# Redrawn issue orders on all five engines of a windowed-attention, depthwise-convolution and MLP block

## The chip, the cores and the metric

The kernel runs on one core of a Trainium2 chip. The metric is the device time of one execution in microseconds (us), as the median of several; less is better. TensorE (PE) does the matmuls, VectorE (DVE), ScalarE (ACT) and GpSimd (POOL) the elementwise work, SyncE (SP) issues most of the DMA transfers. PEld is TensorE's loading of weights, which runs beside its matmuls.

## The reference

The input is 32 images of 96 channels and 56 x 56 pixels. The block is attention in windows of 7 x 7 tokens with 12 heads of 8 channels, a residual sum, a depthwise 3 x 3 convolution with batch norm, and an MLP with 384 hidden channels and a second residual sum.

```python
xw = x.reshape(B, C, 8, 7, 8, 7) ...        # windows of 49 tokens
xn = layernorm(xw) * g + b
q, k, v = xn @ qkv_w.T + qkv_b
attn = softmax(q * SCALE @ k.T + bias)      # 12 heads, 49 x 49 each
seq = x + (attn @ v) @ proj_w.T + proj_b
seq2 = batchnorm(depthwise_conv3x3(seq))
out = seq2 + gelu(seq2 @ w1.T + b1) @ w2.T + b2
```

## The kernel before

The work is cut into 256 chunks. A chunk is one band of seven image rows: 8 windows, 392 tokens (`CT`). Windows are taken in four pairs, so scores, exponentials and values come in four groups, `p` = 0 to 3. There is no scheduler: each engine has a loop over `STEPS` steps whose body is a list of calls written out by hand, such as `exp_scores(s - 4, 2)`, which in step `s` issues the group for chunk `s - 4`. A chunk that doesn't exist (`real(c)` false) issues nothing. An engine runs its list strictly in that order, and engines wait for each other on semaphores: `wait(eng, s, c)` waits until the event `s` of chunk `c` has come, and `free(eng, ...)` until the last reader of a buffer has finished. The step number of one engine has no fixed relation to that of another; only the waits tie them.

What one chunk issues on TensorE, with the line that records it:

- `centred` (L255, writes `d_ps`) and `variance` (L363, `b_ps`): the LayerNorm as two fp32 matmul groups; ScalarE squares (L533) between them, and takes logarithm and root behind them (L540, L547). VectorE multiplies (`input_normal`, L810), ScalarE and GpSimd split the result into two fp16 parts (`input_high` L555, `input_low` L599).
- `queries` (L255, `a_ps`), `keys` (L255, `b_ps`), `values` (L266 to L268, `a_ps`): three fp16 products each. ScalarE and VectorE evict queries and keys as high and low parts (`query_high`, `key_high`, `query_low`, `key_low`), and SP lays them out by six transfers a chunk (`term`, L213).
- `max_scores` (L320, `sm_ps`, four groups): scores whose row maxima VectorE takes (`maxima`, L738). `maxima_rows` (L329) transposes the maxima, VectorE copies them out (`maxima_out`, L748) and SP places them (`maximum_row`, L225).
- `exp_scores` (L299, `st_ps`, four groups): the scores again, transposed, with the maximum subtracted; ScalarE takes the exponential (`exp`, L474).
- `values_times_p` (L345, `o_ps`, four groups): values times exponentials. ScalarE evicts two groups at a time (`outputs`, L499), GpSimd issues four transfers (`to_channels`, L637), ScalarE inverts the sums and VectorE multiplies (`normalise`, L755).
- `projection` (L399, `b_ps`); VectorE adds the residual (`image_sum`, L820). The convolution's nine taps follow, two on GpSimd and seven on VectorE (`tap`, L764).
- `hidden` k = 0, 1, 2 (L266 to L268 into `d_ps`, `a_ps`, `b_ps`), `gelu` on ScalarE (L525), and `second` k = 0, 1, 2 (L255), which accumulates in `d_ps`; VectorE adds up the output (`block_out`, L801) and SP stores it (`store`).

Each of the score and value groups is 24 matmul records with 24 weight loads, 49 columns wide each: 48 instructions. The long groups have few: `centred` 8, `variance` 4, `projection` 8, `keys` and `queries` 12 each, one `hidden` 6, one `second` 8, `values` 24, `maxima_rows` 2. The three scalar calls of a step that need the exponential's table and the three that need the GELU's are separated by two table loads (L560, L574).

`st_ps` and `sm_ps` (two banks each) have one home, so a group of scores can be issued only when the one before it has been read. `a_ps`, `b_ps`, `d_ps` (one bank each) go round between the long groups.

Of the kernel before, what the change touches and what calls it, by code (L numbers as in the profile page):

```python
# [33 lines left out]
STEPS = CHUNKS + 11  # L34
# [4 lines left out]
def block_program(nc, x, w_qkv, b_qkv_row, b_v, w_proj, w_proj_rows, b_proj, ln_g, ln_b, bias_q,  # L39
                  conv_w, bn_g, bn_b, bn_mean, bn_var, w1, b1, w2, b2, eye, low, half, out):  # L40
    ctx = ExitStack()
    with ctx:
# [138 lines left out]
        def _(sp):  # L181
# [51 lines left out]

            for s in range(STEPS):
                load(s)
                first_term(k_all, 0, kh, kh_done, s - 3)
                term(k_all, 2, kh, kh_done, s - 3)
                term(q_all, 0, qh, qh_done, s - 3)
                term(q_all, 2, ql, ql_done, s - 3)
                term(k_all, 1, kl, kl_done, s - 3)  # L240
                term(q_all, 1, qh, qh_done, s - 3)
                store(s - 11)
                maximum_row(s - 4)
# [5 lines left out]
        def _(pe):  # L249
# [82 lines left out]
            def values_times_p(c, p):  # L332
                if not real(c):
                    return
                if p == 0:
                    wait(pe, v32_done, c)
                wait(pe, p_done[p], c)
                if p == 0:
                    free(pe, (o_done[1], c-1), (o_done[0], c-1))
                elif p == 2:  # L340
                    free(pe, (o_done[0], c), (o_done[1], c-1))
# [62 lines left out]
            def hidden(c, k):  # L404
# [3 lines left out]
                if k == 0:  # L408
# [9 lines left out]
            def second(c, k):  # L418
# [6 lines left out]
                halves(d_ps[0:128, 0:CT], w2_s[:, k, :], g[:, k, :], start=k == 0, stop=k == 2).then_inc(s_done[k], 1)  # L425

            for s in range(STEPS):
                exp_scores(s - 4, 2)
                max_scores(s - 3, 3)
                projection(s - 6)  # L430
                hidden(s - 8, 0)
                maxima_rows(s - 3)
                hidden(s - 8, 1)
                hidden(s - 8, 2)
                exp_scores(s - 4, 3)
                max_scores(s - 2, 0)
                second(s - 8, 0)
                second(s - 8, 1)
                second(s - 8, 2)
                keys(s - 1)  # L440
                max_scores(s - 2, 1)
                queries(s - 1)
                exp_scores(s - 3, 0)
                centred(s)
                max_scores(s - 2, 2)
                exp_scores(s - 3, 1)
                values_times_p(s - 4, 2)
                values_times_p(s - 4, 3)
                variance(s)
                values(s - 2)  # L450
                values_times_p(s - 3, 0)
                values_times_p(s - 3, 1)
# [4 lines left out]
        def _(act):  # L457
# [34 lines left out]
            def outputs(c, half):  # L492
# [3 lines left out]
                wait(act, pv_done[1 if half == 0 else 3], c)  # L496
# [5 lines left out]
            def key_high(c):  # L502
# [3 lines left out]
                wait_ring(act, exp_in, c - 2, 6 * 16)  # L506
# [4 lines left out]
            def query_high(c):  # L511

                if not real(c):
                    return
                wait(act, q_done, c)
# [381 lines left out]
```

## Time and profile before

| | |
|---|---|
| median of 3 runs | 3189.77 us (3189.08 to 3205.73) |
| the profiled execution | 3164.1 us |
| its span, first to last instruction | 3162.3 us |
| busy: PE, DVE, ACT, POOL | 96%, 91%, 88%, 62% |
| first and last transpose of maxima (L329), one a chunk | 66.1 and 3104.1 us |

The busy share says how much of the span an engine had an instruction in flight; instructions overlap on an engine, so the sum of the durations of its instructions is above its busy time. "issue" as a reason for idleness means that the engine waited for nothing that the profile shows: no semaphore and no transfer of the program.

### The profile page before, as it was taken

How to read it: one execution, taken by the hardware profiler on the slowest of the kernel's cores; microseconds unless marked ns; L12 is line 12 of the kernel's file. 1: busy time of each engine (PE TensorE's matmuls, PEld its weight loads, DVE VectorE, ACT ScalarE, POOL GpSimd, SP SyncE). 2: the span in 40 equal slices, each digit the busy share in tenths (PEclk: the TensorE clock that was granted, in tenths of full speed). 3: DMA queues.
4: the chain of work that ended last, by engine and by line, in shares of the span. 5: the costliest groups of instructions: out<-in, count | busy, mean ns of one | idle time of the engine just before them, and what ended most of it. 6: DMA issues, size and time to landing. Idle time of an engine off the chain costs nothing.

```text
span 3162.3 us, 199772 instructions
## 1 busy us (share of the span) xinstructions
PE 3029.4 (96%) x88076; PEld 2105.9 (67%) x88076; DVE 2888.8 (91%) x4908; ACT 2768.5 (88%) x4867; POOL 1956.6 (62%) x2574
## 2 busy tenths in 40 slices
PE   3899999999999999999999999999999999999997
PEld 2666666666766666666666666666666676666663
DVE  4799999999999999999999999999999999999996
ACT  2799999989989999998989999988989999998986
POOL 2566666666666666666666666666666666666664
PEclk9999999999999999999999999999999999999998
DMA  1233333333333333333333333333333333333331
GB/s 40 86 91 96 91 96 94 92 95 91 97 91 94 95 94 95 96 91 95 91 96 94 94 96 94 92 96 91 95 95 93 96 97 93 95 98 91 95 92 41
DMA packets 269922, 288.31 MB, mean 91 GB/s; under 512 B 55651, under 2 KB 252580, under 8 KB 269062
## 3 DMA queue, kind: packets, MB, share of 16 engines
q1 hardware_dynamic: 236294, 198.40, 22.6%
q0 software_dynamic: 32768, 77.14, 7.0%
q8 instruction: 700, 11.47, 1.5%
q14 instruction: 160, 1.31, 0.1%
HBM read 39.34 MB, written 38.54 MB: 25 GB/s over the span
## 4 chain that ended last, share of the span: by engine, by line
PE 91%; issue 3%; ACT 2%; SPq 1%; DMA 1%; DVE 1%; POOL 0%; POOLq 0%; ACTq 0%; DVEq 0%
PE d_ps L255 21%; PE st_ps L299 12%; PE o_ps L345 11%; PE sm_ps L320 10%; PE b_ps L363 7%; PE b_ps L399 6%; PE a_ps L255 4%; PE b_ps L255 4%; PE a_ps L266 3%; PE a_ps L268 3%; PE a_ps L267 3%; PE d_ps L266 1%; PE d_ps L268 1%; PE b_ps L267 1%; PE d_ps L267 1%
## 5 line engine op out<-in xcount | busy, mean ns | idle before, releaser
L764 DVE SCALAR_TENSOR_TENSOR s<-ximg,cols,s 96x392 f32<-96x392 f32 x1792 | 1137.0, 635 | 30.7 <-POOL s L627 3.2
L738 DVE TENSOR_REDUCE mx<-sm_ps 128x12 f16<-128x588 f32 x1024 | 785.0, 767 | 127.7 <-PE sm_ps L320 125.1
L474 ACT ACTIVATE p<-st_ps 128x588 f32<-128x588 f32 x1024 | 672.4, 657 | 179.2 <-PE st_ps L299 176.1
L637 POOL DMA_DIRECT2D ox<-o_sb x1024 | 582.7, 572 | 30.8 <-ACT o_sb L499 17.2
L320 PEld LDWEIGHTS sm_ps<-k_all,q_all 127*49 127x49 f16 x24576 | 460.6, 104 | 171.5 <-issue 76.0
L255 PE MATMUL d_ps<-g,w_s 128*64 128x392 f32 x3072 | 560.2, 500 | 0.0
L299 PEld LDWEIGHTS st_ps<-q_all,k_all 128*49 128x49 f16 x24576 | 435.5, 103 | 157.2 <-issue 107.8
L610 POOL TENSOR_TENSOR s<-ximg,cols 96x392 f32<-96x392 f32 x256 | 216.0, 844 | 520.5 <-DVE y L801 519.9
L299 PE MATMUL st_ps<-q_all,k_all 128*49 128x49 f16 x24576 | 516.1, 186 | 21.4 <-issue 19.3
L320 PE MATMUL sm_ps<-k_all,q_all 127*49 127x49 f16 x24576 | 508.6, 186 | 25.9 <-issue 15.6
L599 POOL TENSOR_TENSOR xl<-xn,xh 96x392 f16<-96x392 f32 x256 | 258.8, 1011 | 273.6 <-ACT xh L555 256.5
L645 POOL CAST sh<-s 96x392 f16<-96x392 f32 x256 | 199.5, 779 | 350.0 <-DVE s L764 350.0
L345 PE MATMUL o_ps<-p,v 128*32 128x49 f32 x24576 | 384.9, 209 | 15.2 <-issue 13.1
L345 PEld LDWEIGHTS o_ps<-p,v 128*32 128x32 f32 x24576 | 308.9, 110 | 48.8 <-issue 18.8
L560 ACT ACT_TABLE_LOAD x256 | 328.4, 1283 | 4.5
L574 ACT ACT_TABLE_LOAD x256 | 328.4, 1283 | 4.4
L255 PEld LDWEIGHTS d_ps<-g,w_s 128*64 128x64 f32 x3072 | 197.2, 137 | 197.0 <-ACT g L525 116.0
L791 DVE TENSOR_TENSOR v<-a_ps,half_c 128x768 f32<-128x768 f32 x256 | 245.1, 958 | 36.1 <-PE a_ps L268 16.2
L627 POOL TENSOR_TENSOR s<-s,part 96x392 f32<-96x392 f32 x256 | 261.2, 1020 | 0.1
L652 POOL TENSOR_TENSOR sl<-s,sh 96x392 f16<-96x392 f32 x256 | 239.8, 937 | 20.5
L255 PE MATMUL d_ps<-x_sb,center 96*64 96x392 f32 x1024 | 224.1, 516 | 20.9 <-DMA x_sb<-in_x 20.9
L399 PE MATMUL b_ps<-ox,wp 96*96 96x196 f32 x1024 | 233.3, 350 | 6.3 <-DVE ox L755 5.6
(122 smaller groups left out, 5959.7 us busy)
## 6 DMA issues: line engine op xcount, KB each, us to landing
ox<-o_sb POOLq DMA_DIRECT2D x1024, 73.5 KB
k_all<-kh SPq DMA_DIRECT2D x512, 75.0 KB
q_all<-qh SPq DMA_DIRECT2D x512, 75.0 KB
x_sb<-in_x SPq DMA_DIRECT2D x256, 147.0 KB, 2.4
out<-y SPq DMA_DIRECT2D x256, 147.0 KB, 2.7
q_all<-ql SPq DMA_DIRECT2D x256, 75.0 KB
k_all<-kl SPq DMA_DIRECT2D x256, 75.0 KB
q_all<-mxt SPq DMA_DIRECT2D x256, 9.4 KB, 2.1
```

What stands on the lines that cost most here:

```text
L255: last = mm(o[64 * h:64 * h + 64], w[:, 64 * h:64 * h + 64], m, start=start, stop=stop)
L299: last = mm(st_ps[64 * w:64 * w + TOK, h // HH, c0:c0 + TOK], k_all[:, r, h, n:n + TOK], q_all[:, r, h, n:n + TOK], start=True, stop=True)
L320: last = mm(sm_ps[64 * w:64 * w + TOK, h // HH, c0:c0 + TOK], q_all[0:MAXROW, r, h, n:n + TOK], k_all[0:MAXROW, r, h, n:n + TOK], start=Tr ...
L345: last = mm(o_ps[32 * c4:32 * c4 + 32, at:at + TOK], v32[:, c % 2, h, p, :], p32[:, p, h, :], start=True, stop=True)
L399: last = mm(o, wp[:, 0:C], ox[:, c % 2, w, :].rearrange("c (n r k) -> c n r k", n=NP, k=WS), start=True, stop=True)
L474: af(p32[:, p, :, :].rearrange("p (b h) n -> p b h n", b=2), st_ps[:, :, 0:HALF].rearrange("p b (h n) -> p b h n", n=TOK), ACT.Exp).then_i ...
L560: act.preload_act_table_set("natural_log_exp_and_others")
L574: act.preload_act_table_set("gelu_and_others")
L627: tt(acc, acc, image(part[:, :]), ALU.add).then_inc(tap_done[1], 1)
L637: nc.gpsimd.dma_start(ox[:, c % 2, x4, :], o_sb[x4::4, c % 2, :, :]).then_inc(o_in[c % 2], 16)
L738: v.tensor_reduce(mx[:, c % 2, 0:HEADS, p].rearrange("p (b h) -> p b h", b=2), sm_ps[:, :, 0:HALF].rearrange("p b (h n) -> p b h n", n=TOK ...
L764: v.scalar_tensor_tensor(acc, image_rows(c, k // 3, k % 3), cw_c[:, k:k + 1], acc, ALU.mult, ALU.add)\
```

## The change

The five lists are drawn up anew. On TensorE the eight score groups and the four value groups are spread between the long groups in another order; `values_times_p` takes its pairs in the order 3, 2 and 1, 0; the accumulation in `d_ps` takes `second` in the order 0, 2, 1, with the last of them in the step after; `values` comes before `variance`. The waits move with them (`v32_done` and `o_done` at p = 1 and 3, `pv_done[0]` and `[2]`, `sl_done` at k = 1, `s_done[1]`, the wait for `exp_in` from `key_high` to `query_high`). ScalarE, GpSimd, VectorE and SP get orders and step offsets that go with it. No operation is added or removed, and no shape or buffer changes; `hidden` keeps its PSUM homes.

```diff
...
 CROW = WS * PAD
-STEPS = CHUNKS + 11
+STEPS = CHUNKS + 9
 UP = 256.0
...
             for s in range(STEPS):
+                first_term(q_all, 0, qh, qh_done, s - 2)
+                store(s - 9)
+                term(q_all, 1, qh, qh_done, s - 2)
+                term(k_all, 2, kh, kh_done, s - 2)
+                term(q_all, 2, ql, ql_done, s - 2)
+                term(k_all, 1, kl, kl_done, s - 2)
+                term(k_all, 0, kh, kh_done, s - 2)
                 load(s)
-                first_term(k_all, 0, kh, kh_done, s - 3)
-                term(k_all, 2, kh, kh_done, s - 3)
-                term(q_all, 0, qh, qh_done, s - 3)
-                term(q_all, 2, ql, ql_done, s - 3)
-                term(k_all, 1, kl, kl_done, s - 3)
-                term(q_all, 1, qh, qh_done, s - 3)
-                store(s - 11)
-                maximum_row(s - 4)
+                maximum_row(s - 3)
             for r in stored:
...
                     return
-                if p == 0:
+                if p == 1:
                     wait(pe, v32_done, c)
                 wait(pe, p_done[p], c)
-                if p == 0:
+                if p == 1:
                     free(pe, (o_done[1], c-1), (o_done[0], c-1))
-                elif p == 2:
+                elif p == 3:
                     free(pe, (o_done[0], c), (o_done[1], c-1))
...
                     return
-                if k == 0:
+                if k == 1:
                     wait(pe, sl_done, c)
...
                     free(pe, (g_done[0], c), (xn_done, c+7), (y_done, c-1))
-                halves(d_ps[0:128, 0:CT], w2_s[:, k, :], g[:, k, :], start=k == 0, stop=k == 2).then_inc(s_done[k], 1)
+                halves(d_ps[0:128, 0:CT], w2_s[:, k, :], g[:, k, :], start=k == 0, stop=k == 1).then_inc(s_done[k], 1)
...
             for s in range(STEPS):
-                exp_scores(s - 4, 2)
-                max_scores(s - 3, 3)
-                projection(s - 6)
-                hidden(s - 8, 0)
-                maxima_rows(s - 3)
-                hidden(s - 8, 1)
-                hidden(s - 8, 2)
-                exp_scores(s - 4, 3)
-                max_scores(s - 2, 0)
-                second(s - 8, 0)
-                second(s - 8, 1)
-                second(s - 8, 2)
-                keys(s - 1)
                 max_scores(s - 2, 1)
                 queries(s - 1)
+                second(s - 8, 1)
                 exp_scores(s - 3, 0)
+                keys(s - 1)
+                max_scores(s - 2, 2)
+                values_times_p(s - 4, 3)
+                values_times_p(s - 4, 2)
                 centred(s)
-                max_scores(s - 2, 2)
                 exp_scores(s - 3, 1)
-                values_times_p(s - 4, 2)
-                values_times_p(s - 4, 3)
+                values(s - 2)
                 variance(s)
-                values(s - 2)
+                exp_scores(s - 3, 2)
+                max_scores(s - 2, 3)
+                values_times_p(s - 3, 1)
                 values_times_p(s - 3, 0)
-                values_times_p(s - 3, 1)
+                projection(s - 5)
+                hidden(s - 7, 1)
+                maxima_rows(s - 2)
+                hidden(s - 7, 0)
+                hidden(s - 7, 2)
+                exp_scores(s - 3, 3)
+                max_scores(s - 1, 0)
+                second(s - 7, 0)
+                second(s - 7, 2)
...
                     return
-                wait(act, pv_done[1 if half == 0 else 3], c)
+                wait(act, pv_done[0 if half == 0 else 2], c)
                 if half == 0:
...
                     return
-                wait_ring(act, exp_in, c - 2, 6 * 16)
                 wait(act, k_done, c)
...
                     return
+                wait_ring(act, exp_in, c - 2, 6 * 16)
                 wait(act, q_done, c)
...
             for s in range(STEPS):
-                gelu(s - 8, 2)
                 if real(s - 8):
...
                 exp(s - 4, 3)
-                key_high(s - 1)
                 query_high(s - 1)
...
                 log_sums(s - 5)
+                key_high(s - 1)
+                inverses(s - 5)
                 square(s)
-                inverses(s - 5)
                 exp(s - 3, 1)
...
                 log_variance(s)
+                exp(s - 3, 2)
                 root(s)
-                exp(s - 3, 2)
                 if real(s - 7):
                     act.preload_act_table_set("gelu_and_others")
+                gelu(s - 7, 1)
                 gelu(s - 7, 0)
+                input_high(s)
+                gelu(s - 7, 2)
                 outputs(s - 3, 0)
-                input_high(s)
-                gelu(s - 7, 1)
...
             for s in range(STEPS):
+                second_product(s - 6)
                 first_product(s - 6)
-                second_product(s - 6)
                 image_high(s - 7)
...
                 wait(dve, v_done, c)
-                wait(dve, pv_done[3], c - 2)
+                wait(dve, pv_done[2], c - 2)
                 v.tensor_tensor(v32[:, c % 2, :, :, :].rearrange("p h n (d x) -> p (h n d) x", x=4)[:, :, 0:2],
...
                     return
-                wait(dve, s_done[2], c)
+                wait(dve, s_done[1], c)
                 dve.wait_ge(stored[c % 2], (c // 2 + 1) * 16)
...
             for s in range(STEPS):
-                maxima(s - 2, 2)
+                key_low(s - 1)
+                tap(s - 7, 7)
+                tap(s - 7, 8)
+                normalise(s - 5)
                 values_out(s - 2)
+                maxima(s - 2, 3)
                 input_normal(s)
-                maxima(s - 2, 3)
                 image_sum(s - 5)
...
                 tap(s - 6, 5)
+                maxima(s - 1, 1)
                 tap(s - 6, 6)
                 block_out(s - 7)
-                maxima(s - 1, 1)
-                key_low(s)
                 query_low(s)
-                tap(s - 6, 7)
-                tap(s - 6, 8)
-                normalise(s - 4)
+                maxima(s - 1, 2)
...
```

## Rows read from the trace of the kernel before

**Rows 1.** The page: busy time and share of each engine; the queue of instruction packets.

```profile
PE 3029.4 (96%) x88076; PEld 2105.9 (67%) x88076; DVE 2888.8 (91%) x4908; ACT 2768.5 (88%) x4867; POOL 1956.6 (62%) x2574
...
q8 instruction: 700, 11.47, 1.5%
```

**Rows 2.** Line L329, one matmul a chunk: duration min/median/max, first and last start.

```profile
L329 PE MATMUL sm_ps<-eye_h,mx x256: 219/221/343, 66.1 to 3104.1; 128*96 128x128 f16 x128
```

**Rows 3.** The page, groups: busy, mean ns | idle before, releaser.

```profile
L299 PE MATMUL st_ps<-q_all,k_all 128*49 128x49 f16 x24576 | 516.1, 186 | 21.4 <-issue 19.3
L320 PE MATMUL sm_ps<-k_all,q_all 127*49 127x49 f16 x24576 | 508.6, 186 | 25.9 <-issue 15.6
...
L345 PE MATMUL o_ps<-p,v 128*32 128x49 f32 x24576 | 384.9, 209 | 15.2 <-issue 13.1
```

**Rows 4.** Timeline of PE over one chunk: start, duration, engine, line, operation.

```profile
1512.70 0.33 PE L268 MATMUL b_ps<-sh,w_l 96*128 96x392 f16 x1
1512.96 0.50 PE L299 MATMUL st_ps<-q_all,k_all 128*49 128x49 f16 x24
...
1513.63 2.17 PE L255 MATMUL d_ps<-g,w_s 128*64 128x392 f32 x12
...
1517.31 0.86 PE L255 MATMUL d_ps<-x_sb,center 96*64 96x392 f32 x4
1518.00 0.49 PE L320 MATMUL sm_ps<-k_all,q_all 127*49 127x49 f16 x24
1518.32 0.48 PE L299 MATMUL st_ps<-q_all,k_all 128*49 128x49 f16 x24
1518.73 0.73 PE L345 MATMUL o_ps<-p,v 128*32 128x49 f32 x48
1519.39 0.90 PE L363 MATMUL b_ps<-sq,avg 96*96 96x392 f32 x2
1520.13 0.21 PE L266 MATMUL a_ps<-wq_h,xh 96*128 96x96 f16 x1
...
1520.59 0.21 PE L268 MATMUL a_ps<-wq_h,xl 96*128 96x96 f16 x1
1520.73 0.73 PE L345 MATMUL o_ps<-p,v 128*32 128x49 f32 x48
1521.39 0.50 PE L299 MATMUL st_ps<-q_all,k_all 128*49 128x49 f16 x24
...
1522.14 0.90 PE L399 MATMUL b_ps<-ox,wp 96*96 96x196 f32 x4
1522.88 0.33 PE L266 MATMUL d_ps<-sh,w_h 96*128 96x392 f16 x1
...
1524.53 0.24 PE L299 MATMUL st_ps<-q_all,k_all 128*49 128x49 f16 x4
```

**Rows 5.** Timeline of PE at a pause in a score group, 1545 to 1547 us.

```profile
1545.35 0.34 PE L320 MATMUL sm_ps<-k_all,q_all 127*49 127x49 f16 x13
1546.49 0.29 PE L320 MATMUL sm_ps<-k_all,q_all 127*49 127x49 f16 x9 [0.79 <-issue]
```

**Rows 6.** DMA queues from 1543.5 to 1543.7 us: packets, MB, share of 16 engines.

```profile
q8 instruction: 1, 0.02, 44.8%
```

**Rows 7.** Timeline of ACT over the same chunk.

```profile
1511.05 1.28 ACT L574 ACT_TABLE_LOAD   x1
...
1515.91 0.66 ACT L474 ACTIVATE p<-st_ps 128x588 f32<-128x588 f32 x1
...
1520.33 0.58 ACT L540 ACTIVATE sq<-b_ps,cols 96x392 f32<-96x392 f32 x1
1520.94 0.53 ACT L547 ACTIVATE sq<-sq 96x392 f32<-96x392 f32 x1
```

**Rows 8.** Timeline of DVE: residual sum, and the maxima that end the stretch.

```profile
1511.52 0.62 DVE L820 SCALAR_TENSOR_TENSOR ximg<-b_ps,cols,x_sb 96x392 f32<-96x392 f32 x1
...
1513.91 0.76 DVE L738 TENSOR_REDUCE mx<-sm_ps 128x12 f16<-128x588 f32 x1
```

## The prediction

> **What bounds the kernel now.** I read the page first. TensorE is busy for 96% of the span, the others for less [rows 1]; busy is not the same as running at its best, so I went on to the spacing of the groups. The transposes of the maxima come once a chunk: (3104.1 - 66.1) / 255 = 11.91 us for a chunk [rows 2]. Then the timeline of TensorE over one chunk in which nothing is late: from one fourth exponential group to the next, 1512.96 to 1524.53, are 11.57 us, and every group starts as soon as the one before it lets it [rows 4]. So 0.34 us of a chunk, 88 us of the run, are pauses, and the rest is the list itself. The groups of the page say what the pauses are: of 21.4, 25.9 and 15.2 us of idle time before score and value matmuls, 19.3, 15.6 and 13.1 are "issue", no semaphore and no transfer of the program [rows 3]. (The modelled ends hide about 0.2 us of each pause, so these 48 us stand for most of the 88.)
>
> One pause shows the cause. A group of maximum scores stops after 13 of its 24 matmuls and goes on 0.79 us later, at 1546.49 [rows 5]; a matmul in the middle of a group has nothing of the program to wait for. Between 1543.5 and 1543.7 an instruction packet starts; its 44.8% of 16 engines over 0.2 us are 1.4 us of transfer [rows 6]. The queue carries 700 packets and 11.47 MB, 16 KB each [rows 1]. TensorE's 176,152 matmuls and weight loads and some 3,000 semaphore instructions make 700 times 256. So a packet is a block of 256 instructions. I count 256 back from the restart: 26 of this group, 48, 96, 24, 4, and 58 of the 96 of `values_times_p`. By the pitches of [rows 4] that stretch would take 0.18 + 0.34 + 0.66 + 0.60 + 0.74 + 0.40 = 2.9 us; it took 3.9. I read it so: a new block is asked for when the block before is entered, and is ready some 3.1 to 3.9 us later. A stretch of 256 instructions that the array could do faster than that ends in a pause. The mean block has 11.91 / 2.73 = 4.4 us; the dense ones don't.
>
> The Trainium skill ("Runtime: NRT & Kernel Launch", Instruction fetch mechanics) says that instructions are refilled in 16 KiB blocks of 256, which the queue's packets agree with, and that crossing a block's edge is mostly hidden, which the 0.79 us above speaks against. It is a rival below.
>
> **The change, part by part.** Nothing is added or removed, so only order counts.
>
> *Dense stretches.* Before, `max_scores` 2, `exp_scores` 1, `values_times_p` 2 and 3, `variance`, `values`, `values_times_p` 0 and 1, `exp_scores` 2 and `max_scores` 3 follow each other: 412 instructions from 1518.00 to 1522.14, 4.14 us [rows 4], which is 2.6 to 2.9 us for any 256 of them. Now `centred`, `exp_scores` 1, `values`, `variance`, `exp_scores` 2, `max_scores` 3, `values_times_p` 1 and 0 make the densest stretch. From `exp_scores` 1 on, 256 instructions (48, 24, 4, 48, 48, 84 of 96) take 0.41 + 0.54 + 0.81 + 0.34 + 0.41 + 0.57 = 3.1 us; those from `max_scores` 2 on take 3.7, all others more. I slide a window of 256 instructions over the 700 starts of a chunk's list, each group's time spread evenly over its instructions. Before, 36% of the starts lie below 3.3 us, and 700 blocks lose 95 us at a refill of 3.3 us (46 at 3.1, 176 at 3.6). The 88 us measured fit 3.27. The same sliding over the new list gives 11% of the starts and 12 us at 3.3 (3 at 3.1, 40 at 3.6). As refills scatter, I take 17 us, with 5 and 40 as ends. Gain 71 us (48 to 83).
>
> *Edges between groups.* TensorE pays when it goes from one width of output to another. I call A the groups on 64 columns (scores, `centred`, `queries`, `keys`, `second`), B those on 32 (`values_times_p`), C those on 96 or 128. From [rows 4]: C to A costs 0.26 - 0.17 = 0.09 and 0.02 in the group behind; A to B 0.41 - 0.32 = 0.09; B to C 0.74 - 0.66 = 0.08; C to B 0.60 for twelve matmuls that start (1520.59 - 1520.13) / 11 = 0.042 apart, 0.10; B to A 0.02; A to C 0.75 + 0.74 against 0.66 + 0.66, 0.17. Each stands once in the old list: 0.57. The new list has A-B (`max_scores` 2), B-A (`centred`), A-C (`exp_scores` 1 to `values`), C-A (`variance` to `exp_scores` 2), A-B (`max_scores` 3), B-C (`projection`) and C-A (`hidden` 2): seven edges. A-C into fp16 is not in the trace: 0.09 to 0.17, between which I take 0.13. `variance` behind `values` isn't either: its fp32 weights load behind matmuls of 0.04 us, 0 to 0.08, I take 0.04. Sum 0.09 + 0.02 + 0.13 + 0.04 + 0.11 + 0.09 + 0.08 + 0.11 = 0.67. `second` in two pieces pays its start twice: one pair of halves like `centred` takes 0.69 to the next group, each further pair (2.17 - 0.86) / 2 = 0.655, so 0.03. The list without pauses is 11.57 + 0.67 - 0.57 + 0.03 = 11.70 us (11.62 to 11.78): 256 x 0.13 = 33 us lost (12 to 54).
>
> *Waits that could reach TensorE.* I laid the new lists beside each other at 11.70 us with `max_scores` 1 at 0. Three places have little room.
> ScalarE: from `variance` (5.07) the way goes back to `exp_scores` 0 of the next step. Start of `variance` to the logarithm 0.94 [rows 4, 7]; logarithm to the exponential group behind it 0.47 to 0.61; this group and the root 0.55 each; from the first table load to the exponentials behind the second 4.86, as the same three GELUs, one output eviction and `input_high` stand between them in both lists [rows 7]; the exponential group 0.66 and a semaphore 0.05. That is 8.08 to 8.22, and 8.35 if the group behind the logarithm takes its full 0.66 and more. TensorE's own list from `exp_scores` 0 to `variance` is 3.56. The loop is 11.64 to 11.78, at worst 11.91, beside TensorE's 11.70.
> VectorE: `projection` starts at 7.27; its result is there 0.95 later; `image_sum`, `tap` 2, `maxima_out`, `tap` 3 and 4 take 2.39, `maxima` 0 another 0.76, and 0.05 [rows 8]: 4.15 us, and `max_scores` 1, which needs it, comes 4.42 us after `projection`. Spare 0.27. VectorE is busy 2888.8 / 256 = 11.3 us of a chunk [rows 1], so it stays under 11.70 but has nothing to give.
> GpSimd and SP: `input_low` ends some 0.5 us before `queries`. SP blocks in order: behind `maximum_row`'s wait stand the next chunk's six transfers, but their data comes 4 us later, so nothing is held up; with some 0.7 us an issue, and the store now ahead of five of them, the last of the six still goes out about 4 us before `max_scores` 0 needs it. The load of x goes out 5 us earlier relative to its use.
> For all of these I add 5 us (0 to 30, the end where the loop is 11.80).
>
> *Pipeline depth.* `STEPS` falls by two, but this renumbers more than it shortens. From `centred` to the transpose were 3 steps less 5.4 us, now 2 steps and 5.1; from there to the last `second` 5 steps and 3.8, now 5 and 4.7. Both within 1 us: 0, with 8 either way.
>
> *Sum.* -71 + 33 + 5 + 0 = -33 us. The profiled execution took 3164.1 us (a span of 3162.3 and 1.8 around it), so 3131 by its own time. The median of the runs is 3189.8, 0.8% above; taking the difference over as it is, I predict 3157 us.
>
> **The rivals.**
> *1. The ScalarE loop sets the pace, slower.* It would replace the pauses by a wait of `exp_scores` 0 for `exp` 3. For it: the loop is within 0.1 us of TensorE's list at the lower rows, 11.91 at the highest. Against: ACT has idle time before a chunk's `exp` groups now, and is busy 2768.5 / 256 = 10.8 us [rows 1]. At 11.91 with 0.07 of pauses it is 11.98, and 256 x 0.07 = +18 us, 3208. From a loop of 11.91 on it ends as slower than 3206.
> *2. The pauses stay.* The Trainium skill's rule on block edges stands beside this one: if an edge of a block were hidden, the issue time would have another cause, which the order would not touch. As a mechanism of this kernel: the pauses come at the same rate, 88 us, and the edges add 33: 3223. Against: the pause in the middle of a group and the count of 256.
> *3. Everything is used up.* The high ends of both: refills so slow that the pauses fall by only 48, edges that take 54, waits 5: 3201, no change to speak of.
> *4. More than I say.* The low ends of both, the edges and the refill: -83 + 12: 3119.
>
> **How the numbers follow.** Less than 0.5% (16 us) is about what a measurement of this kernel can't tell from no change. The forecast with rival 4, below 3174, 0.65; rival 3 and mixtures that end between 3174 and 3206, 0.18; rival 1 0.09; rival 2 0.08. The forecast's own range is 3127 to 3180, from the ends of its terms short of all falling together. For 8 in 10 the range goes down to rival 4 and up past rival 1: 3115 to 3210.
>
> **What would show it.** Right: transposes 11.75 to 11.80 us apart; undisturbed chunks at 11.62 to 11.78; "issue" before L299, L320 and L345 well under half of 48 us; `values` to `variance` and `exp_scores` 2 as costed. Wrong: `exp_scores` 0 waiting for `exp` (L474), `max_scores` 1 for `maxima` (L738), `queries` for `input_low` (L599), or issue time as before.

## The result: 1.3% slower, and the profile after

The changed kernel takes 3234.9 us (median of 4 runs, 3229.1 to 3241.6) where the kernel before takes 3191.9 on the same chip: 1.0127, 95% interval [1.009, 1.0163]. The profiled execution took 3229.1 us, 65.0 more than the one of before. The forecast was 3157 us and faster. A second measure of the same kernel on another occasion (a_again below) gave 1.014. The page of the changed kernel:

```profile
PE 3065.0 (95%) x88076; PEld 2093.7 (65%) x88076; DVE 2871.7 (89%) x4908; ACT 2745.1 (85%) x4867; POOL 2039.4 (63%) x2574
...
q8 instruction: 700, 11.47, 1.6%
...
L299 PE MATMUL st_ps<-q_all,k_all 128*49 128x49 f16 x24576 | 522.9, 186 | 31.3 <-issue 27.2
L320 PE MATMUL sm_ps<-k_all,q_all 127*49 127x49 f16 x24576 | 510.3, 185 | 30.0 <-DMA k_all<-kh 12.2
...
L345 PE MATMUL o_ps<-p,v 128*32 128x49 f32 x24576 | 382.3, 209 | 22.6 <-issue 21.5
```

Beside [rows 1, 3]: the same 700 instruction packets. TensorE and GpSimd are busy for longer (3065.0 us beside 3029.4, 2039.4 beside 1956.6), VectorE and ScalarE for less, and as a share of the span none moved by more than three points. The issue time before exponential scores rose from 19.3 to 27.2 us and before values from 13.1 to 21.5. The prediction wanted well under half of 48. The transposes, from the query on L329:

```profile
L329 PE MATMUL sm_ps<-eye_h,mx x256: 219/221/257, 65.7 to 3169.2; 128*96 128x128 f16 x128
```

(3169.2 - 65.7) / 255 = 12.17 us a chunk, against 11.91 [rows 2]. Head and tail of the run are as before (65.7 and 58.1 us beside 66.1 and 58.2), so the whole loss lies between them. First, a chunk in which nothing is late (timeline of TensorE):

```profile
660.09 0.22 PE L329 MATMUL sm_ps<-eye_h,mx 128*96 128x128 f16 x1
...
665.58 0.50 PE L320 MATMUL sm_ps<-k_all,q_all 127*49 127x49 f16 x24
666.01 0.73 PE L345 MATMUL o_ps<-p,v 128*32 128x49 f32 x48
666.67 0.88 PE L255 MATMUL d_ps<-x_sb,center 96*64 96x392 f32 x4
667.38 0.49 PE L299 MATMUL st_ps<-q_all,k_all 128*49 128x49 f16 x24
667.80 0.22 PE L266 MATMUL a_ps<-wq_h,xh 96*128 96x96 f16 x1
...
668.32 0.86 PE L363 MATMUL b_ps<-sq,avg 96*96 96x392 f32 x2
669.11 0.50 PE L299 MATMUL st_ps<-q_all,k_all 128*49 128x49 f16 x24
669.45 0.48 PE L320 MATMUL sm_ps<-k_all,q_all 127*49 127x49 f16 x24
669.86 0.73 PE L345 MATMUL o_ps<-p,v 128*32 128x49 f32 x48
670.52 0.90 PE L399 MATMUL b_ps<-ox,wp 96*96 96x196 f32 x4
...
671.76 0.22 PE L329 MATMUL sm_ps<-eye_h,mx 128*96 128x128 f16 x1
```

671.76 - 660.09 = 11.67 us; the kernel before has 11.56 at its best. So the edges between groups cost 0.11 x 256 = 29 us, where 33 were forecast for them and the two pieces of `second`: `values` to `variance` 0.52, `variance` to `exp_scores` 2 0.79, the whole list within 0.03 of the 11.70 on record. That part was right.

The rest is 12.17 - 11.67 = 0.50 us a chunk that is not in the list, where before it was 0.36. To split it I went through TensorE's records in order (matmuls, weight loads, semaphore instructions) and cut them into blocks of 256. In both traces the unexplained gaps in the middle of groups fall on one fixed remainder, the first instruction of a block. A "pause" below is what the spacing at such an edge of a block has over the same place in undisturbed chunks, and a block is "entered" when the array starts its first instruction. Summed over all edges the pauses are **86 us before (189 of them) and 103 us after (188)**; 94 in the second execution of the changed kernel. The forecast was 17. Besides, waits for transfers of k_all and q_all, for `input_low` and for `maxima` rose: in TensorE's waits those for `k_all` (12.2), `q_all` (0.9), `xl` (10.1) and `mx` (6.7 and 1.1) make 31 us, and before 16. List 29, pauses 17 and these 15 make 61 of the 65 us.

What the new pauses look like. This is TensorE's timeline around the worst kind, then the one row of ScalarE there, then the queues from 1750.4 to 1750.6 us:

```profile
1747.94 0.48 PE L320 MATMUL sm_ps<-k_all,q_all 127*49 127x49 f16 x24
...
1748.78 0.83 PE L255 MATMUL d_ps<-g,w_s 128*64 128x392 f32 x4
1749.47 0.50 PE L299 MATMUL st_ps<-q_all,k_all 128*49 128x49 f16 x24
...
1750.31 0.50 PE L320 MATMUL sm_ps<-k_all,q_all 127*49 127x49 f16 x24
1750.74 0.72 PE L345 MATMUL o_ps<-p,v 128*32 128x49 f32 x47
1753.17 0.20 PE L345 MATMUL o_ps<-p,v 128*32 128x49 f32 x1 [1.70 <-issue]
```

```profile
1748.67 0.66 ACT L474 ACTIVATE p<-st_ps 128x588 f32<-128x588 f32 x1
```

```profile
q8 instruction: 1, 0.02, 40.8%
```

The block that ends in this pause began in `max_scores` 1, at about 1748.05 (counted back from the pause: 94 instructions of `values_times_p`, 48 of `max_scores` 2, 12 of `keys`, 48 of `exp_scores` 0, 8 of `second`, 12 of `queries`, some six semaphore instructions, and the last 28 of `max_scores` 1). The next packet starts in 1750.4 to 1750.6: some 2.4 us after the block was entered, where in [rows 5, 6] it was about 1. It takes 0.408 x 16 x 0.2 = 1.3 us, and work goes on 1.4 us after it has landed, as elsewhere. Late is only its start. And that start lies 1.1 us behind the end of the exponential of group 3 (1748.67 + 0.66 = 1749.33), for which `exp_scores` 0 waits, some 50 instructions behind the first of the block. That exponential is rival 1's. It costs the array nothing here: `exp_scores` 0 starts at 1749.47, on the heels of `second`.

### The profile page after: what moved, and what is told of

The parts are those of the page before. It is cut to its first block, busy times and chain, and to the rows that moved or that the text cites. A ratio compares the mean times of both kernels' runs of the same rounds, so it can differ in the third digit from the quotient of the medians.

```text
span 3227.3 us, 199772 instructions
## 1 busy us (share of the span) xinstructions
PE 3065.0 (95%) x88076; PEld 2093.7 (65%) x88076; DVE 2871.7 (89%) x4908; ACT 2745.1 (85%) x4867; POOL 2039.4 (63%) x2574
## 4 chain that ended last, share of the span: by engine, by line
PE 86%; issue 4%; DMA 3%; SPq 3%; ACT 2%; DVE 2%; POOL 1%; POOLq 0%; ACTq 0%; DVEq 0%
PE d_ps L255 21%; PE st_ps L299 11%; PE o_ps L345 10%; PE sm_ps L320 10%; PE b_ps L399 6%; PE b_ps L363 5%; PE a_ps L255 4%; PE b_ps L255 4%; PE a_ps L266 3%; PE a_ps L268 2%; PE a_ps L267 2%; DMA k_all<-kh 2%; SPq L213 2%; PE d_ps L266 1%; PE d_ps L267 1%
## 5 line engine op out<-in xcount | busy, mean ns | idle before, releaser
L299 PEld LDWEIGHTS st_ps<-q_all,k_all 128*49 128x49 f16 x24576 | 447.4, 103 | 495.1 <-issue 330.0
L255 PE MATMUL d_ps<-g,w_s 128*64 128x392 f32 x3072 | 603.7, 500 | 0.1
L299 PE MATMUL st_ps<-q_all,k_all 128*49 128x49 f16 x24576 | 522.9, 186 | 31.3 <-issue 27.2
L320 PE MATMUL sm_ps<-k_all,q_all 127*49 127x49 f16 x24576 | 510.3, 185 | 30.0 <-DMA k_all<-kh 12.2
L345 PE MATMUL o_ps<-p,v 128*32 128x49 f32 x24576 | 382.3, 209 | 22.6 <-issue 21.5
L599 POOL TENSOR_TENSOR xl<-xn,xh 96x392 f16<-96x392 f32 x256 | 270.7, 1058 | 159.1 <-ACT xh L555 150.8
L345 PEld LDWEIGHTS o_ps<-p,v 128*32 128x32 f32 x24576 | 307.4, 110 | 37.9 <-issue 18.0
L618 POOL TENSOR_TENSOR part<-ximg,cols 96x392 f32<-96x392 f32 x256 | 289.0, 1129 | 0.2
L533 ACT ACTIVATE sq<-d_ps 96x392 f32<-96x392 f32 x256 | 126.0, 492 | 148.8 <-PE d_ps L255 148.8
```

What stands on the lines that cost most here:

```text
L255: last = mm(o[64 * h:64 * h + 64], w[:, 64 * h:64 * h + 64], m, start=start, stop=stop)
L299: last = mm(st_ps[64 * w:64 * w + TOK, h // HH, c0:c0 + TOK], k_all[:, r, h, n:n + TOK], q_all[:, r, h, n:n + TOK], start=True, stop=True)
L320: last = mm(sm_ps[64 * w:64 * w + TOK, h // HH, c0:c0 + TOK], q_all[0:MAXROW, r, h, n:n + TOK], k_all[0:MAXROW, r, h, n:n + TOK], start=Tr ...
L345: last = mm(o_ps[32 * c4:32 * c4 + 32, at:at + TOK], v32[:, c % 2, h, p, :], p32[:, p, h, :], start=True, stop=True)
L599: tt(xl[0:C, c % 2, :, 0:TOK], xn[:, :, :], xh[0:C, c % 2, :, 0:TOK], ALU.subtract).then_inc(xl_done, 1)
L618: tt(image(part[:, :]), image_rows(c, 0, 1), weight(1), ALU.mult).then_inc(part_done, 1)
```

## The experiments

Pauses in the table are counted as above, from one trace a kernel; two traces of the same kernel gave 103 and 94 us, so a difference of some 10 us is not one. "List" is the undisturbed chunk. Each ratio is to the kernel before on the same chip; names with b_ are edits of the kernel before, with a_ of the changed one.

| kernel | ratio, 95% interval | list, us | pauses at edges of blocks, us (number) |
|---|---|---|---|
| before | 1 | 11.56 | 86 (189) |
| changed | 1.0127 [1.009, 1.0163] | 11.67 | 103 (188) |
| a_again | 1.014 [1.0114, 1.0165] | 11.67 | 94 (184) |
| b_thin | 0.9808 [0.9787, 0.9829] | 11.55 | 32 (68) |
| a_thin | 0.9914 [0.989, 0.9937] | 11.72 | 9 (20) |
| b_lite | 0.9959 [0.9942, 0.9976] | 11.56 | 86 (193) |
| a_lite | 1.0107 [1.0081, 1.0133] | 11.67 | 92 (168) |
| a_thin1 | 1.0449 [1.0421, 1.0478] | 11.68 | 187 (270) |
| a_thin2 | 0.9934 [0.9908, 0.9959] | 11.69 | 19 (48) |
| b_thin2 | 0.9856 [0.9826, 0.9886] | 11.56 | 56 (122) |
| a_thin1_notab | 0.9938 [0.9914, 0.9962] | 11.65 | 39 (77) |
| a_notab | 0.9934 [0.9916, 0.9952] | 11.65 | 40 (76) |
| b_notab | 1.0137 [1.0116, 1.0158] | 11.56 | 130 (233) |
| a_swap | 1.0064 [1.0041, 1.0086] | 11.65 | 77 (131) |
| b_low | 0.999 [0.9975, 1.0006] | 11.56 | 94 (207) |
| b_notab_low | 0.9932 [0.991, 0.9953] | 11.56 | 92 (200) |
| a_swap2 | 0.9951 [0.9935, 0.9967] | 11.65 | 47 (111) |
| a_swap2_again | 0.9988 [0.9974, 1.0002] | 11.65 | 49 (104) |
| b_later | 1.0645 [1.0621, 1.067] | 12.50 | 53 (119) |

**Is it the number of instructions? b_thin and a_thin.** In every `max_scores` group four matmuls of 384 columns stand for 24 of 49, so 8 instructions for 48 in the same time; the maxima are of other products then, and the exponential's scale is 0.01. In both kernels:

```
-                for h in range(HEADS):
+                for b in range(2):
                     for w in range(2):
...
+                        last = mm(sm_ps[64 * w:64 * w + TOK, b, 0:384], q_all[0:MAXROW, r, b, n:n + TOK],
+                                  k_all[0:MAXROW, r, b, 0:384], start=True, stop=True)
```

> The kernel before, but each max_scores group is 4 matmuls of 384 columns (8 instructions) in the place of 24 of 49 (48 instructions), about the same 0.32 us of the array; the maxima are of other scores, and the exponential is taken of a hundredth of its argument. A chunk has 540 instructions, not 700. Refill theory (pauses come when TensorE runs through a block of 256 instructions faster than the next arrives): a block lasts 5.6 us on the mean, nearly all pauses go, 11.6 us a chunk, 3060 to 3100 us by the profiled time. Rival, the pauses have another cause (waits, edges of groups): 3140 to 3165 as before.

> The changed kernel with the same thinning of max_scores. Refill theory: pauses nearly gone here too, what is left is the undisturbed list, 11.67 us a chunk in its own trace against 11.56: 3085 to 3125 us by the profiled time, 25 to 40 us above the thinned kernel before, so about 80 of the change's 110 us of pauses and list are pauses. Rival, the new lists wait on ScalarE or VectorE: it stays above 3180.

Pauses fell from 86 to 32 and from 103 to 9 us with a list unchanged in one and 0.05 longer in the other. TensorE's waits of a_thin show hardly any issue time left:

```profile
PE st_ps L299 <- issue: 3.5, 10, 0.6
```

The profiled execution of b_thin took 3104.7 us, 5 above its expectation, that of a_thin 3144.9, 20 above: TensorE's waits for k_all (12.5 us) and for `input_low` (13.7 us) stay in a_thin. The pauses are refills in both kernels, against rival 2; what is wrong is the size they were given.

**Is it the traffic that slows a packet? b_lite and a_lite.** The transfers of the terms move one of eight windows; the rest of the scores' operands stays as it was set at the start.

```
-                sp.dma_start(t[n:TERMS:4, c % 4, :, :], part[:, c % 2, :]).then_inc(exp_in[c % 4], 16)
+                sp.dma_start(t[n:TERMS:4, c % 4, :, 0:KP], part[:, c % 2, 0:KP]).then_inc(exp_in[c % 4], 16)
```

> The kernel before with the six transfers of queries and keys a chunk moving one of eight windows (9 KB each in the place of 75); the other windows' scores are those of the initial tables. Traffic theory (the instruction packet waits behind and beside the program's own transfers): refills shorten by 0.3 us or more and most of the 88 us of pauses go: 3090 to 3110. Density theory (the packet needs its time whatever else moves): at most 20 us less, 3140 to 3160.

> The changed kernel with the same small transfers. Traffic theory, by which the change moved the transfers onto the wrong stretches: most of its 120 us of pauses go, 3110 to 3140, and it comes within 40 us of the kernel before so lightened. Density theory: pauses stay near 100 us, 3200 to 3225.

Pauses 86 and 92: not the traffic, beyond some 10 us. (A packet takes 1.14 us at the median in the changed kernel's trace and 1.01 in a_lite's.)

**Which stretch? a_again, a_thin1, a_thin2, b_thin2.** The thin group is now only `max_scores` 1 or only 2 (`if p == 1:` or `if p == 2:` around the lines above).

> The changed kernel once more, to stand beside the next three and the kernel before on one chip. 1.0 to 1.6% above the kernel before; 11.66 us an undisturbed chunk, and pauses at the edges of instruction blocks near 100 us by its trace.

> The changed kernel with max_scores group 1 alone thinned to 8 instructions of the same array time (maxima of other scores, the exponential of a hundredth of its argument). Edge theory (a refill lasts some 3.9 us for TensorE here, and the pauses come from the 38 to 46% of block starts whose 256 instructions take less; sliding the window over this list at 3.9 gives 92 us in the place of 108): 10 to 25 us less than the changed kernel. Rival, scattered slow refills that any block can meet: the same gain as in a_thin2.

> The changed kernel with max_scores group 2 alone thinned, the group that stands between keys and values_times_p 3 and so lies in most of the blocks of 3.6 to 4.0 us. Edge theory: the window gives 47 us of pauses at 3.9, 50 to 65 us less than the changed kernel and 35 to 50 less than a_thin1, though both leave out the same 40 instructions of a chunk. Rival, scattered slow refills: no more than 10 us apart from a_thin1.

> The kernel before with max_scores group 2 alone thinned, the first of its run of 412 instructions. With the refill of 3.1 to 3.3 us that fits the kernel before, the window gives 22 to 51 us in the place of 46 to 95: 25 to 45 us less than the kernel before. If the true refill there were 3.9 as in the changed kernel, it would be 155 in the place of 270, over 100 us less.

Group 2 went the expected way in both kernels: 67 us less than a_again, beside 50 to 65, and 46 us less than the kernel before, beside 25 to 45. a_thin1 did not: 40 instructions fewer a chunk, no list change, and 84 us **more** pauses than the changed kernel. In its page the pauses stand before the values above all (L352 is the old L345):

```profile
L299 PE MATMUL st_ps<-q_all,k_all 128*49 128x49 f16 x24576 | 530.2, 187 | 41.8 <-issue 38.9
L352 PE MATMUL o_ps<-p,v 128*32 128x49 f32 x24576 | 395.7, 210 | 63.4 <-issue 62.0
```

No theory by density alone can give that, so mine fell. I looked at when packets start. In a_thin1, where the wait of `exp_scores` 0 for the exponential of group 3 lies 8 to 87 instructions behind the first of a block (79 blocks), 63 packets start 0.9 to 1.8 us after that wait has ended (median 1.1), a median of 3.4 us after the block was entered. In blocks without this wait, half of the packets start 1.0 to 1.6 us after the entry. I read it so: **the request for the next block goes out only some way into the present one, and not while TensorE's queue stands at a semaphore.** The array still has work in front of it then, so the wait itself costs nothing; the packet that it holds back does, up to 2.5 us later. The changed kernel has about as many blocks with the wait up to 87 instructions behind their first, but in it far fewer packets follow the wait so; why a_thin1 has more is not shown.

**Take the wait's reason away: a_thin1_notab, a_notab, b_notab.** GELU becomes Identity, and ScalarE's two table loads a chunk go, so that the exponential of group 3 is done 1.57 us before `exp_scores` 0 starts, and not 0.14.

```
-                af(g[:, k, :], ..., ACT.Gelu, bias=b1_c[:, k:k + 1], scale=1 / UP).then_inc(g_done[k], 1)
+                af(g[:, k, :], ..., ACT.Identity, bias=b1_c[:, k:k + 1], scale=1 / UP).then_inc(g_done[k], 1)
...
-                if real(s - 7):
-                    act.preload_act_table_set("gelu_and_others")
```

> a_thin1 (max_scores group 1 thin) without both table loads and with the identity in the place of the GELU, so that ScalarE's fourth exponential group ends some 2.5 us earlier and exp_scores 0 doesn't wait for it. Hold theory, formed after a_thin1 took 98 us more for 40 instructions fewer: the request for the next instruction block goes out only after the sequencer has run some way into the block before; while it is held at a semaphore it asks for nothing, and in that run the packets whose boundary lies 8 to 88 instructions ahead of the wait of exp_scores 0 start 1.0 to 1.3 us after this wait ends, up to 4.2 us after the boundary. By it the 187 us of pauses fall below 80: 3120 to 3190. Density theory (only how fast the 256 instructions are used up counts): no more than 15 us less, above 3300.

> The changed kernel without both table loads and with the identity in the place of the GELU; TensorE's work is the same. Hold theory: the wait of exp_scores 0 for exp 3 is gone and the pauses fall from about 100 to 50 to 70 us: 3170 to 3200, against 3226 in this state of things. Density theory: TensorE's list and its instruction density are unchanged, 3215 to 3230.

> The kernel before with the same left out, as the control. Both theories: TensorE is hardly held at exp_scores 0 here (the wait ends 0.4 us before the group starts), so 0 to 20 us less than the kernel before. If it gains as much as a_notab, the table loads cost TensorE something that has nothing to do with the hold.

TensorE's order and instructions are the same, and the pauses fall from 187 to 39 us and from about 98 to 40. That is within the expectation for a_thin1_notab and better than it for a_notab (50 to 70 us of pauses, 3170 to 3200 us; it took 3159). The page of a_thin1_notab, to be held beside that of a_thin1, and one line of a_notab's:

```profile
L299 PE MATMUL st_ps<-q_all,k_all 128*49 128x49 f16 x24576 | 508.5, 186 | 3.7 <-DMA q_all<-mxt 1.5
L352 PE MATMUL o_ps<-p,v 128*32 128x49 f32 x24576 | 383.1, 209 | 19.1 <-issue 18.7
```

```profile
L299 PE MATMUL st_ps<-q_all,k_all 128*49 128x49 f16 x24576 | 508.7, 186 | 3.8 <-DMA q_all<-mxt 1.9
```

Over the blocks with the wait 8 to 31 instructions behind their entry, the next packet starts a median of 2.2 us after the entry in a_thin1 and 2.0 in the changed kernel, but 1.0 in a_thin1_notab. Counted from the end of the wait it is 1.2 to 1.3 us in all three. So that this wait, cleared too late, makes packets late is shown. Two things limit it. In the kernel before, 18 of 27 packets of such blocks start before the wait has ended or less than 0.5 us behind it, so a wait at this place does not hold every request. And of the 62 us between the changed kernel and a_notab only about 22 lie behind blocks with the wait up to 87 instructions behind their first. Some 30 more lie behind blocks that begin in `exp_scores` 0 or in the 60 instructions behind it. There no wait is left to stand at, but the queue has come past it only just ahead of the array: in blocks that begin in `exp_scores` 0, packets start 0.94 us after the entry in the changed kernel and 0.19 us before it in a_notab. That this lost lead is the reason is argued. ScalarE's other groups come sooner without the table loads as well; that it is this wait rests on a_swap2 below too.

b_notab went the other way, against the expectation of 0 to 20 us less: 46 us more. Its VectorE and GpSimd timelines have this:

```profile
1518.87 2.02 DVE L760 SCALAR_TENSOR_TENSOR s<-ximg,cols,s 96x392 f32<-96x392 f32 x2
```

```profile
1519.57 0.90 POOL L595 TENSOR_TENSOR xl<-xn,xh 96x392 f16<-96x392 f32 x1 [0.22 <-ACT xh L555]
```

A pair of convolution taps takes 2.02 us beside GpSimd's `input_low` (1.27 otherwise, as at 1521.49 in the same chunk). In the kernel before `input_low` ran beside the maxima that read PSUM [rows 8], at 1513.75, and the taps kept 0.6 us each. The Trainium skill ("SBUF — State Buffer", SBUF: two separate sides) says that a VectorE operation with two SBUF inputs and a GpSimd operation that reads SBUF exclude each other for a whole instruction; the 0.75 us extra beside a 0.90 us operation agree with it roughly.

**Keep VectorE and GpSimd apart: b_low, b_notab_low.** `input_low` on one of eight windows, in the kernel before and in b_notab.

```
-                tt(xl[0:C, c % 2, :, 0:TOK], xn[:, :, :], xh[0:C, c % 2, :, 0:TOK], ALU.subtract).then_inc(xl_done, 1)
+                tt(xl[0:C, c % 2, 0:1, 0:TOK], xn[:, 0:1, :], xh[0:C, c % 2, 0:1, 0:TOK], ALU.subtract).then_inc(xl_done, 1)
```

> The kernel before with GpSimd's input_low on one of the eight windows instead of all (the rest of x_low keeps its zeros), the control for the next run. In the kernel before this operation runs beside a maximum reduction and not beside a pair of VectorE's convolution taps, so taps keep 635 ns. Both theories: within 15 us of the kernel before.

> b_notab (no table loads, Identity for GELU) with the same cut of input_low. Theory A (contention, then a held request): in b_notab GpSimd's input_low fell beside a pair of taps, which then took 2.0 us instead of 1.27; centred's input came late, TensorE's sequencer stood at that wait, and the request for the next block went out late. Without the operation the taps are back at 630 to 650 ns and the time is at or under the kernel before: 40 to 90 us less than b_notab, some 3130 to 3185 us beside 3180. Theory B: b_notab is slow for another reason of its changed phases (ScalarE ahead of TensorE, other waits in the dense stretch): it stays within 15 us of b_notab, ratio 1.009 to 1.018.

VectorE's group of taps in b_notab, and in b_notab_low:

```profile
L760 DVE SCALAR_TENSOR_TENSOR s<-ximg,cols,s 96x392 f32<-96x392 f32 x1792 | 1306.2, 729 | 31.1 <-POOL s L623 3.5
```

```profile
L760 DVE SCALAR_TENSOR_TENSOR s<-ximg,cols,s 96x392 f32<-96x392 f32 x1792 | 1139.9, 636 | 31.6 <-POOL s L623 4.1
```

Back to 636 ns, pauses back from 130 to 92 us, ratio from 1.0137 to 0.9932, and in b_low the cut alone does nothing. So the contention is the cause of b_notab's loss. The link behind it, that late taps delay `centred`'s input and its wait holds requests back, fits TensorE's records (the wait is over 8 pairs of instructions or less ahead of the array, 18 before) but was only argued.

**Move the wait: a_swap, a_swap2.** Nothing is left out. `keys` goes ahead of `exp_scores` 0 (a_swap); `max_scores` 2 too (a_swap2, whose edit is shown). In both, `exp` 0 on ScalarE moves behind `log_sums` and `key_high`.

```
                 queries(s - 1)
                 second(s - 8, 1)
-                exp_scores(s - 3, 0)
                 keys(s - 1)
                 max_scores(s - 2, 2)
+                exp_scores(s - 3, 0)
                 values_times_p(s - 4, 3)
```

> The changed kernel with keys ahead of exp_scores 0 on TensorE (and ScalarE's exponential 0 behind log_sums and key_high), nothing left out. Hold theory: exp_scores 0 comes 0.5 us later, its wait holds the sequencer shorter: 10 to 30 us less than the changed kernel. Density theory: three dense groups now stand together (exp_scores 0, max_scores 2, values_times_p), so 10 to 30 us more.

> The changed kernel with exp_scores 0 after keys and after max_scores 2 on TensorE (ScalarE's order as in a_swap). Nothing is left out. The wait for exp 3 then has 0.4 us more room than in a_swap, but the exponential groups 0 and 1 stand nearer to each other. Theory (held request plus density): no hold is left at that wait, so 0 to 20 us less than a_swap, 3180 to 3200 us beside a kernel before of 3180. Rival (the wait's place does not matter, a_swap's gain was the keys group in the dense stretch): within 8 us of a_swap either way.

> The same kernel as a_swap2, for a second measure of it on another occasion. Nothing is left out. If its 0.9951 holds, it comes out between 0.992 and 0.998 of the kernel before.

By the ratios that is 20 to 24 us less than the changed kernel for a_swap and 44 to 60 for a_swap2, pauses 103 to 77 to 48. a_swap2 gained more than the 0 to 20 us over a_swap that were expected, and its second measure, 0.9988, is just outside 0.992 to 0.998. The rival, that the wait's place does not matter, is out. In a_swap2 the exponential, from ScalarE's timeline, and the groups on TensorE:

```profile
1513.34 0.66 ACT L474 ACTIVATE p<-st_ps 128x588 f32<-128x588 f32 x1
```

```profile
1514.62 0.48 PE L320 MATMUL sm_ps<-k_all,q_all 127*49 127x49 f16 x24
1514.94 0.48 PE L299 MATMUL st_ps<-q_all,k_all 128*49 128x49 f16 x24
```

It is done at 1514.00, 0.94 us ahead of `exp_scores` 0 instead of 0.14. In the blocks with the wait 8 to 31 instructions behind their first, packets still start 1.1 us after the wait has ended, but that is now 0.2 us after the entry, and their pauses fall from 12 us to 1. The page:

```profile
L320 PE MATMUL sm_ps<-k_all,q_all 127*49 127x49 f16 x24576 | 505.6, 186 | 30.8 <-DMA k_all<-kh 13.4
L299 PE MATMUL st_ps<-q_all,k_all 128*49 128x49 f16 x24576 | 509.2, 186 | 2.7 <-ACT p L474 1.3
...
L345 PE MATMUL o_ps<-p,v 128*32 128x49 f32 x24576 | 381.5, 209 | 16.8 <-issue 15.6
```

Issue time before exponential scores is gone. The two measures, 0.9951 and 0.9988, put a_swap2 between 16 us under the kernel before and level with it: most of the 38 us of pauses that it has less go into 0.095 x 256 = 24 us of edges and into the waits for transfers that the changed kernel has too.

**The same in the kernel before: b_later.** `exp_scores` 0 behind `centred` and `max_scores` 2.

```
-                exp_scores(s - 3, 0)
                 centred(s)
                 max_scores(s - 2, 2)
+                exp_scores(s - 3, 0)
                 exp_scores(s - 3, 1)
```

> The kernel before with exp_scores 0 after centred and max_scores 2, nothing left out. Its wait for exp 3 then has a full queue ahead instead of 2 pairs, but the two exponential groups now stand side by side, so the dense stretch is 40 instructions longer: the window of 256 slid over the list gives about 20 us more of pauses. Theory A (a held request costs in the kernel before as well): the loss of density is made good, -15 to +10 us. Theory B (in the kernel before density alone makes the pauses): +12 to +35 us.

It took 206 us more, where the two theories ended at +10 and +35, for a plain reason that I had overlooked. All four groups share one home in PSUM (`st_ps`), and `exp_scores` 1 waits for the exponential of group 0. TensorE's waits of b_later:

```profile
PE st_ps L299 <- ACT p L474: 193.7, 257, 0.8
```

Side by side the two groups wait 0.75 us each chunk, 194 us in all, and the run tells nothing of the held request in the kernel before.

## Why the prediction was wrong

*Dense stretches, -71 us: the term that failed.* It rests on the sentence that a block "is ready some 3.1 to 3.9 us later" counted from its predecessor's entry, with one constant: "The 88 us measured fit 3.27." Measured, pauses went from 86 to 103 us, +17. Two things were wrong in it.
First, the time is not a constant, and the value fitted to the old list is that of its densest blocks. Worked out block by block (the packet's start after the entry, its transfer, and 1.40 us from landing to restart), it is 3.50 us at the median before, with half of the blocks between 3.1 and 3.9; in the densest, below 3.1 us undisturbed, it is 3.2, because their packets start 0.74 us after the entry and not 1.03. Of these there were 228 before, and they lost 74 of the 86 us. In the changed kernel only 35 are so dense, as forecast, and lost 28. But 188 now have 3.6 to 4.0 us (10 before). At 3.27 they lose nothing; they lost 44. The old list bunched its density; the new one spreads it, so that many more blocks lie near the edge. The two other lengths that the text tried, 3.1 and 3.6 (3 and 40 us for the new list), show how steep this is, and 40 was taken as the far end.
Second, the late wait. Without it (a_notab, a_swap2) the new list pauses for 40 to 49 us, with it 94 to 103. So about 30 of the error of some 85 us is the first cause, and 50 the second. Put as one constant, the new list fits 3.6 us without the late wait and 3.9 with it, and at 3.9 the same sliding would give the kernel before 265 us where it lost 86: no one length fits both lists.

*Edges, +33:* 29 measured. *Other waits, +5:* 15, within its 0 to 30. *Depth, 0:* right. The sum with the true first term is 17 + 29 + 15 = 61 of 65 us.

*Rival 1* named the right wait, `exp_scores` 0 for `exp` 3, and the wrong price. It was to lengthen the chunk when the loop exceeds TensorE's list; it hardly ever does (1.8 us of TensorE's time are idle for it). It acts while the array does not yet wait for it. *Rival 2* (3223) came nearest in its number, and its reason is refuted by a_thin: the pauses are edges of blocks. That the pauses hardly changed in sum (86 and 103 us) is chance, as far as the runs show: dense blocks became few, and late packets many. The Trainium skill's rule behind it ("Runtime: NRT & Kernel Launch", Instruction fetch mechanics), that crossing an edge is mostly hidden, fits by number only: 511 of the 700 edges before show no pause, but the others cost 86 of 3164 us, and in a_thin1 270 of 660 cost 187 of 3328. *Rivals 3 and 4* assumed a refill of one length, as the forecast did.

*What stays open:* what decides how far into a block the request goes out (held packets have the wait up to 31 instructions behind the entry for the most part in the changed kernel, and up to 87 in a_thin1), and why many with the wait as near are not held; whether `centred`'s wait is the link in b_notab; and how much of the 86 us of the kernel before come from late waits. Only 9 of them lie behind blocks with the wait for `exp` 3 up to 87 instructions behind their first; other waits were not counted.

## What to carry to other kernels

Where a queue of short instructions runs near the rate at which its blocks come, don't fit one refill time to the pauses of the old order: price the new list at the longest refill that the trace shows, and look at how many blocks lie between the fitted and the longest. And ask of each semaphore wait not only whether the array is idle behind it but how far ahead of the array it is cleared; one that comes just in time can make the instructions that follow late. Before two groups are put side by side, look at which buffer they share.

## What the runs showed of the hardware

- A 16 KB instruction packet takes 0.9 to 1.5 us on its queue (changed kernel; median 1.0 before, 1.14 after), and TensorE, where it pauses, goes on 1.3 to 1.6 us after it has landed; the start lies about 1 us behind the entry of the block, and 3.4 us at the median of those that follow the wait in a_thin1.
- A wait that costs the array next to nothing (1.8 us in all) goes with late instruction packets. With it cleared sooner, pauses fell by 54 to 63 us (changed kernel to a_swap2 and a_notab) and by 148 us (a_thin1 to a_thin1_notab).
- Less work made a kernel slower: 40 TensorE instructions fewer a chunk cost 84 us in pauses (a_thin1), and two table loads fewer cost 46 us (b_notab), the latter through a GpSimd operation of 0.90 us that moved beside two VectorE taps and added 0.75 us to them.
